# Early maxima for four heads instead of two, the rest spread evenly over the attention heads, and FFN low parts on GpSimd

## What is computed

```python
xn = layernorm(x)                                   # x: 4 x 2048 x 256
qkv = xn @ W_qkv                                    # 16 heads of 16 numbers
scores = einsum('bhqd,bhkd->bhqk', q, k) + bias     # 2048 x 2048 for each of 64 heads
attn = softmax(scores)
a = einsum('bhqk,bhkd->bhqd', attn, v) @ W_out
gate = sum of the two renormalised router probabilities of a token
f = (gelu(xn @ w1 + b1) @ w2 + b2) * gate
out = x + a + f
```

## Time and profile before

| what | value |
|---|---|
| median of three runs | 3269.54 us |
| the profiled execution: its own time, its span | 3269.68 us, 3267.8 us |
| mean granted TensorE clock | 0.994 |
| TensorE busy | 3200.7 us (98%) |
| VectorE busy | 2813.3 us (86%) |
| ScalarE busy | 2439.0 us (75%) |
| GpSimd busy | 1297.9 us (40%) |
| VectorE, line 1042 (maxima, 2666 groups) | 2398.1 us busy |
| ScalarE, line 960 (exponentials) | 2156.3 us busy |

### The profile page before, as it was taken

How to read it: one execution, slowest core, us unless ns; L and a number is a source line. 1 busy time by engine, 2 the same in 40 slices (tenths; PEclk the granted TensorE clock), 3 DMA queues, 4 the chain that set the end, 5 groups by cost and what they waited for, 6 DMA issues and landing times.

```text
span 3267.8 us, 72368 instructions
## 1 busy us (share of the span) xinstructions
PE 3200.7 (98%) x28170; PEld 1717.4 (53%) x28170; DVE 2813.3 (86%) x3760; ACT 2439.0 (75%) x4667; POOL 1297.9 (40%) x1918
## 2 busy tenths in 40 slices
PE   7999999799999999999999999999999999999997
PEld 6888889344444444444444444444444444444446
DVE  5577765699999999999999999999999999999922
ACT  4443344588888888888888888888888888888883
POOL 1212112344444444444444444444444444444445
PEclk9999999899999999999999999999999999999999
DMA  8532232432222222221122222212222221222105
GB/s 194 123 91 78 78 108 87 78 66 37 37 37 37 37 37 37 37 37 37 37 37 37 37 37 37 37 37 37 37 37 37 37 37 37 37 37 37 23 10 186
DMA packets 136725, 175.46 MB, mean 54 GB/s; under 512 B 53008, under 2 KB 100816, under 8 KB 130048
## 3 DMA queue, kind: packets, MB, share of 16 engines
q1 hardware_dynamic: 136384, 170.83, 25.6%
HBM read 110.31 MB, written 56.69 MB: 51 GB/s over the span
## 4 chain that ended last, share of the span: by engine, by line
PE 77%; DVE 3%; DMA 2%; issue 1%; SPq 0%; POOL 0%; ACT 0%; DVEq 0%; ACTq 0%
PE ps L1108 27%; PE ps L1125 24%; PE ps L1097 18%; PE ps L1130 8%; DVE max_half L1042 2%; DMA out_rows<-base_in 1%; PE ps L1165 0%; DMA k_st<-base_in 0%; DMA base_in<-base_rows 0%; SPq L194 0%; POOL prob L1007 0%; DVE neg_turn L1055 0%; SPq L860 0%; POOL turned L1015 0%; ACT turned L967 0%
## 5 line engine op out<-in xcount | busy, mean ns | idle before, releaser
L1042 DVE TENSOR_REDUCE max_half<-ps 128x1 f32<-128x512 f32 (+1 forms) x2666 | 2398.1, 945 | 121.5 <-PE ps L1097 118.1
L960 ACT ACTIVATE prob<-ps 128x512 f32<-128x512 f32 x4096 | 2156.3, 600 | 440.4 <-PE ps L1108 428.4
L1007 POOL TENSOR_TENSOR prob<-prob,near 128x224 f32<-128x224 f32 (+2 forms) x1664 | 978.3, 603 | 1450.9 <-ACT prob L960 1444.6
L1108 PE MATMUL ps<-q_st,k_st 49*128 49x512 f32 x4096 | 1407.3, 442 | 21.4 <-DMA k_st<-base_in 21.1
L1097 PE MATMUL ps<-k_st,q_st 48*128 48x512 f32 x3968 | 1403.2, 450 | 8.5 <-DVE max_half L1042 7.1
L1108 PEld LDWEIGHTS ps<-q_st,k_st 49*128 49x128 f32 x4096 | 658.8, 184 | 747.3 <-ACT prob L960 681.1
L1125 PE MATMUL ps<-prob,vr 128*32 128x384 f32 x4864 | 756.3, 498 | 0.0
L1097 PEld LDWEIGHTS ps<-k_st,q_st 48*128 48x128 f32 x3968 | 636.9, 184 | 180.7 <-DVE max_half L1042 103.3
L1125 PE MATMUL ps<-prob,vx 128*32 128x384 f32 x3328 | 593.5, 499 | 1.1 <-issue 1.1
L1125 PEld LDWEIGHTS ps<-prob,vr 128*32 128x32 f32 x4864 | 133.4, 108 | 325.5 <-issue 221.4
L662 PE MATMUL ps<-xnt,w_parts 128*128 128x512 f32 x1152 | 275.4, 398 | 8.7 <-DVE parts L512 5.1
(11 more groups left out here) (70 smaller groups left out, 1161.6 us busy)
## 6 DMA issues: line engine op xcount, KB each, us to landing
qk_parts<-parts SPq DMA_DIRECT2D x64, 512.0 KB, 4.7
q_st<-qk_parts SPq DMA_DIRECT2D x192, 128.0 KB, 3.9
k_st<-qk_parts SPq DMA_DIRECT2D x192, 128.0 KB, 5.4
near<-bias_near SPq DMA_DIRECT2D x64, 352.0 KB, 6.2
x_sb<-in_L_attn_hidden_states SPq DMA_DIRECT2D x18, 512.0 KB, 6.1
base_rows<-x_sb SPq DMA_DIRECT2D x16, 512.0 KB, 2.9
recip_rows<-recip_all SPq DMA_DIRECT2D x256, 32.0 KB, 1.8
base_in<-base_rows SPq DMA_DIRECT2D x16, 512.0 KB, 5.7
```

The costliest lines, as they stand in the source:

```text
L960: nc.scalar.activation(prob[:, t % PROBS, CH * j:CH * (j + 1)], ps[:, bank_of(at)], ACT.Exp).then_inc(drained, 1)
L1007: nc.gpsimd.tensor_tensor(at, at, near[n % GROUP][:, side, c0:c0 + q1 - q0], ALU.mult).then_inc(near_done, 1)
L1042: nc.vector.tensor_reduce(max_half[:, m % 2].rearrange("p i c -> p (i c)")[:, k:k + len(banks)], tiles, AX.X, ALU.max) \
L1108: nc.tensor.matmul(ps[:, bank_of(at)], k_st[u][:, P * kb:P * (kb + 1)], q_st[u][:, CH * c:CH * (c + 1)], start=True, stop=True).then_inc(s ...
```

## The change

**Four heads in the first phase.** Pieces of heads 0 and 1 stand in batch 1, those of heads 2 and 3 in batch 2, 16 in each of the eight early chunks. They stand after three of the q/k products, in the first FFN product after blocks 1, 3, 5 and 7, after the second v product, and eight in the second FFN product. The first eight of a chunk use banks 0 and 1, the last eight banks 4 and 5.

**FFN low parts on GpSimd.** The eight subtractions of line 529 leave VectorE's list and stand in GpSimd's (`hid_lows`), with the power -1/2 after the third. VectorE's normalisation stands one block later.

**An even stream.** `max_groups` now hands out the 3840 maxima tiles of heads 4 to 63 over all score slots up to visit 13 of head 62: three in most visits, two in about every eighth, 61 a head. Combining a head's maxima and turning them comes one and two visits after its last tile, wherever in a head that is. The reductions are 2528 groups (1312 of two, 1216 of one) instead of 2666 (1302 and 1364). The score ring has three banks to the end.

**Stacks of their own.** Two stacks for scores (partitions 0 to 48) and two for maxima (64 to 111), loaded apart: twelve stack DMAs a head instead of six. `neg_turn` holds six heads' rows. SyncE's order in head n is now: score stacks of head n+1; the row of head n+1 if its maxima were turned before head n began (heads n up to 45); stacks for maxima whose time came in the last visits of head n-1; bias table; sums and reciprocals of head n-1; stacks for maxima (ends in visits 0 to 8); `keep`; stacks for maxima (ends in visits 9 to 14); and the row of head n+1 where it did not stand above (heads n from 46 to 62, 17 of them).

```diff
-    for m in range(LEAD, NH):
-        k = 0
-        for v, visit in enumerate(VISITS):
-            for size in ([2, 1] if len(visit) == WIDE else [1] * len(visit)):
...
+    wanted, slots = CPB * KB * (NH - EARLY_HEADS), CPB * KB * (NH - 1) - sum(len(visit) for visit in VISITS[NV - SPARE:])
+    passed = done = 0
+    for t in range(NV * NH):
+        passed = min(passed + len(VISITS[t % NV]), slots)
+        take = wanted * passed // slots - done
+        tiles = []
+        while take > 0:
+            m, k = EARLY_HEADS + done // (CPB * KB), done % (CPB * KB)
+            size = min(take, 2, CPB * KB - k)
+            at = len(groups)
+            choices = [range(bank, bank + size) for bank in range(CPB + 1 - size)]
+            banks = min(choices, key=lambda taken: sorted((freed[bank] for bank in taken), reverse=True))
...
+                def hid_lows(n):
+                    for f in range(KF):
+                        if f == 3:
+                            norm(n + 1)
+
+                        wait(pool, hid_high, KF * n + f + 1)
+                        if f == 0:
+                            wait(pool, f2_ready, TPC * n)
+                        nc.gpsimd.tensor_tensor(hid[:, 1, f], hid_raw[:, f % RAWS], hid[:, 0, f].bitcast(F32), ALU.subtract).then_inc(hid_low, 1)
...
                 def early_scores(b, c, piece):
 
-                    i, j = early_block(b, c, piece)
-                    wait(pe, max_done, early_first(b, c) + piece)
+                    i, j = early_block(c, piece)
+                    bank = 0 if piece < EARLY_F2 else 4
+                    if piece == EARLY_F2:
+                        wait(pe, gelu_done, KF * (CPB * b + c + 1))
+                    elif piece > 0:
+                        wait(pe, max_done, early_first(b, c) + piece)
...
+                def load_max(m):
+
+                    if m - STACKS >= EARLY_HEADS:
+                        sp.wait_ge(max_ready, max_end(m - STACKS))
+                    load_stacks(sp, m, q_max[m % STACKS], k_max[m % STACKS], max_in[m % STACKS])
+
+                def load_maxima(first, last):
+
+                    for m in range(EARLY_HEADS + STACKS, NH):
+                        if first <= MAX_ENDS[m - STACKS][0] < last:
+                            load_max(m)
...
                 for n in range(NH):
-                    if n + GROUP - 1 < NH:
-                        load(n + GROUP - 1)
-                        load_near(n + GROUP - 1)
+                    early_turn = n + 1 < NH and turned_in(n + 1) < NV * n
                     if n + 1 < NH:
+                        load(n + 1)
+                    if early_turn:
                         shift(n + 1)
+                    load_maxima(NV * (n - 1) + NORM_AT, NV * n)
+                    if n + NEARS - 1 < NH:
+                        load_near(n + NEARS - 1)
                     if n > 0:
                         totals(n - 1)
                         spread(n - 1)
+                    load_maxima(NV * n, NV * n + TOTAL_AT)
+                    if n > 0:
                         keep(n - 1)
+                    load_maxima(NV * n + TOTAL_AT, NV * n + NORM_AT)
+                    if n + 1 < NH and not early_turn:
+                        shift(n + 1)
...
                     for v, visit in enumerate(VISITS):
                         if v == 0:
 
-                            pe.wait_ge(shift_in[n % GROUP], 16 * SHIFT_LOADS * (n // GROUP + 1))
...
+                            pe.wait_ge(shift_in[n % STACKS], 16 * SHIFT_LOADS * (n // STACKS + 1))
+                            pe.wait_ge(score_in[n % STACKS], 16 * STACK_LOADS * (n // STACKS + 1))
```

More of the change, by code:

```diff
@@ L40 @@
 HALF = 64
-GROUP = 4
-GROUPS = NH // GROUP
-LEAD = 2
+STACKS = 2
+NEARS = 4
+NEGS = 6
 PROBS = 4
@@ L309, in transformer_layer @@
             gate_step = sem("gate_step")
-            early_in = sem("early_in")
+            early_in = [sem(f"early_in{i}") for i in range(EARLY_PASSES)]
             W_LOADS = 2
@@ L513, in chunk @@
                             .then_inc(lo_done, 1)
-                        if early and m == EARLY_QK:
-                            early_max(b, c, 0)
+                        if early and m in EARLY_QK:
+                            early_max(b, c, EARLY_QK[m])
                     if not first:
@@ L533, in chunk @@
                             w_low_part(W_2)
+                        if early and f in EARLY_F1:
+                            early_max(b, c, EARLY_F1[f])
+                    if early:
+                        early_max(b, c, EARLY_VR[1])
                     wait(dve, r_copied, TPC * (n + 1))
@@ L633, in _ @@
                     chunk(0, c)
-                for b in range(1, B - 1):
+                for b in range(1, B):
                     for c in range(CPB):
                         chunk(b, c)
-                act.wait_ge(max_done, EARLY)
-                for c in range(CPB):
-                    chunk(B - 1, c)
             @block.tensor
@@ L688, in chunk @@
                             .then_inc(qk_ready, 1)
-                        if early and m == EARLY_QK:
-                            early_scores(b, c, 0)
+                        if early and m in EARLY_QK:
+                            early_scores(b, c, EARLY_QK[m])
                     for f in range(KF):
+                        if f == 0 and (early or c == 0 and b > 0):
+                            wait(pe, max_done, early_first(b, c))
                         if f in (2, 3):
@@ L700, in chunk @@
                             .then_inc(f1_ready, 1)
+                        if early and f in EARLY_F1:
+                            early_scores(b, c, EARLY_F1[f])
                     for t in range(TPC):
@@ L710, in chunk @@
                             .then_inc(vr_ready, 1)
+                        if early and t in EARLY_VR:
+                            early_scores(b, c, EARLY_VR[t])
                     if early:
-                        wait(pe, max_done, early_first(b, c) + 1)
+                        wait(pe, max_done, early_first(b, c) + EARLY_F2)
                     transposes(n + 1)
```

247 lines of the change are left out of this document (123 added, 124 removed).

## The result

| | before | after |
|---|---|---|
| median of the runs | 3269.65 us (3268.29 to 3270.3) | 3382.19 us (3369.08 to 3399.55, 4 runs) |
| ratio, 95% interval | | 1.0348 (1.0301 to 1.0395) |
| profiled execution, its span | 3269.68, 3267.8 us | 3369.08, 3367.3 us |
| mean granted clock, profiled run (all runs) | 0.994 | 0.979 (0.979, 0.977, 0.974, 0.970) |
| first score tile | 594.3 us | 673.5 us |

What follows compares the result with a forecast made beforehand. TensorE was taken to bound both phases, with VectorE a close second in the heads. The terms 58 + 0 - 63 + 34 + 5 = +34 us on 3269.68 us gave 3304 us, range 3250 to 3335.

Steps and rivals of the forecast that it cites:

- Eight more pieces, +58: First phase, eight early chunks: the added pieces' TensorE work, +39 us, and waits for reductions, +19 us.
- piece 4: Early chunks: TensorE waits 1.3 us there for the reduction of piece 3, standing behind VectorE's other work.
- Low parts on GpSimd, 0: First phase: eight subtractions at 1.2 us and the power fit beside TensorE's eight hidden blocks, so 0 us.
- the port rule: Trainium skill: GpSimd and a VectorE instruction with two SBUF inputs share a port pair; whichever starts second is blocked.
- rival (c): First phase: GpSimd becomes the chunk's bound; at 1.8 us a subtraction, 16 chunks grow some 3 us each: 3350 us; chance 0.08.
- Even stream, -63: Second phase: hand-overs of maxima banks fewer or cheaper, 40 us where 104 stood, with smaller terms -63 us.
- the +5 for loads: Some dozen heads up to 45: maxima's loads ahead of the sums' DMAs, +5 us (0 to 15).
- Late row, +34: Heads 47 to 63: bias row behind `keep`, 0.5 us late in 13 heads, 7 us in four: +34 us.
- (d): Second phase: hand-overs keep their price, the even stream brings -30 instead of -63 us, 3337 us; chance 0.10.

Runs made afterwards that it cites:

- x7: The kernel of x1 with GpSimd writing zeros in place of the subtraction for the hidden blocks' low parts: 3276.42 us, ratio 1.0032.
- x1: The changed kernel with the bias row's four DMAs ahead of the results' eight in heads 47 to 63: 3299.58 us, ratio 1.0099.
- x11: The kernel before with only the low parts on GpSimd and the normalisation one block later: 3287.37 us, ratio 1.0057.
- x12: The kernel before with the second phase's reductions reading 64 columns of each bank instead of 512: 3081.57 us, ratio 0.9423.
- x2: The changed kernel with the bias row's DMAs still behind the results' eight, but ahead of six stack loads in heads 57 to 60: 3344.40 us, ratio 1.0214.
- x6: The kernel before with the single tile ahead of the pair in every second visit of three maxima tiles: 3217.99 us, ratio 0.9854.
- x8: The kernel of x1 with early chunks' pieces moved and VectorE's reductions of pieces 2, 3, 4 ahead of statistics, variance and normalisation: 3277.24 us, ratio 1.0039.
- x10: The kernel before with every maxima tile of the second phase a group by itself: 3142.38 us, ratio 0.9609.

## Why the prediction was wrong, step by step

- **Eight more pieces, +58: right.** "What the profile after would show" said 44 us for an early chunk. Without the port conflict (x7) it is 43.74, and the first score tile of x7 stands at 646.0 us, 51.7 behind before's. The waits are where the working had them, at the second, fifth and tenth piece: 0.52, 1.07 and 0.31 us in x7 where it had 0.65, 1.3 and 0.4. The fifth ("piece 4") is doubled in after by the step that follows.
- **Low parts on GpSimd, 0: the step that failed in the first phase.** The prediction had the port rule, and in that paragraph the very wait, at piece 4, growing by up to a subtraction's length; it grew by 1.6 us. But it put the term at 0, because a power of 4 elements beside a base row showed nothing, and where it gave the rule a price, in rival (c) at 0.08, it had GpSimd late, and not VectorE's short instructions, which take GpSimd's time each. Measured: 23 us in the changed kernel (x1 against x7), 17 us alone (x11). In all the first phase grew by 79 us: 52 without the conflict (the pieces' own work and the waits of their order), 23 with it, and 4.6 between after's and x1's executions of the same first phase.
- **Even stream, -63: wrong in its ground.** "TensorE's own work is about 39.1 us a head" took for TensorE's own what was still hand-over. TensorE's own is 37.77 (x12), and the hand-over costs 3.0 us a head and not 1.7. Lead of VectorE was to make a hand-over cost 0.1 us instead of 0.24; but a tile waits for a bank held through a pair's 1.22 us, whatever the lead. Measured -41 (x1), of which 4 from evenness; with the +5 for loads, which no run separates, -58 had been predicted.
- **Late row, +34: the mechanism right, the price of it too small.** The waits came in the heads named, 39.1 us of TensorE's time, 30.6 of them at the ends of heads 57 to 60 where the working had 28. The term that failed is one that the sum didn't have, TensorE's clock, which fell to half in six stretches with those waits: with it the late heads took 61.5 us more in the profiled run, and by the medians of x1 and after the row cost 83.
- **The sum.** By x1's and after's profiles: 79.2 - 41.4 + 63.1 (late heads: 2624.6 - 2561.5) - 1.4 = 99.5 us. The 13 us from there to the median of after are runs at a lower mean clock (0.974 and 0.970 the lowest); a profile of one execution didn't show them.
- **The rivals.** (c) had the port conflict but not its way; (d) was right that the stream brought less, for another reason. No case held two terms at once, and the range ended at 3335 because errors of the terms were taken singly.

What stays open: what makes the clock fall behind one wait and not behind another. It fell behind four of six waits of 2.7 us in after's early chunks, the runs of x2 differ by 33 us, and x6 has two stretches of 3.4 us at half clock inside heads where TensorE had no idle time over 0.15 us. How far below 43 us an early chunk would come with x8's order and no conflict was not run, and neither were more banks for the maxima in place of smaller groups.

## What to carry to other kernels

Before a share of time is called an engine's own work, take the other engine's work away in one run (here: 64 columns instead of 512) and see what is left. A period that two engines share can be neither's own: a visit took 1.81 us where VectorE alone would need 1.74, and a head took 3.0 us less once VectorE's work was cut. Read the cost of small instructions from runs of them without a gap, not from their mean length; where they hold a buffer of which there are few, the smaller group can win although it is more instructions. The Trainium skill says as much ("Perfetto Trace Analysis", "Optimizing Scalar/DVE Operations": breaking up instructions may let work complete sooner), though for engines that are not saturated; VectorE here was 86% busy, and x10 is faster with VectorE nearly without a gap. A wait on TensorE is to be counted with what the clock does behind it.

## What the runs showed of the hardware

- VectorE's one- and two-input instructions from SBUF and GpSimd's subtraction of 512 elements take turns, one for one, and only VectorE's get longer (5.33 us for four `xn`, 1.31 us a subtraction, x11); writing zeros on GpSimd leaves them nearly as they were (0.467 instead of 0.407 us for `xn`, 0.479 for a base row, x7), and a reduction out of PSUM beside a subtraction keeps its length (1.21 us, after).
- Reductions of 512 columns out of PSUM follow each other every 0.60 us, of 1024 every 1.14 us, while their rows say 0.67 to 0.68 and 1.22 us.
- After a wait of 2.69 us in the first phase TensorE ran 3.4 us at half clock (a granted 0.50), though not after each such wait; with waits of 1.1 to 8.2 us at heads' starts it ran 10 to 24 us at half clock (after); and one program (x2), with waits of at most 1.4 us in its profiled run, ran at a mean of 0.993 or of 0.982.
